# Attention and feed-forward block on one core: the next group's weights are prepared by a table of slots

## What is computed

```python
ln = layernorm(layernorm(x)) * ln_w + ln_b
q, k, v = fp8_linear(ln, wq), fp8_linear(ln, wk), fp8_linear(ln, wv)   # each input divided by its scale, clipped, rounded to fp8
qx      = fp8_linear(ln, wqx)
kx, vx  = split(ctx @ w_kv_x.T)                                        # cross attention on the context
q, k, qx, kx = ln_over_128_columns(each head)
core = softmax(q k^T / sqrt(128)) v ;  xout = softmax(qx kx^T / sqrt(128)) vx   # 8 groups, 2 heads of each kind in a group
x = x + fp8(concat(core, xout) / proj_smooth) @ wproj.T * scales
x = x + (silu(z @ gate.T) * (z @ up.T)) @ down.T,  z = layernorm(x)    # int weights, zero point 128
```

## Time and profile before

| | |
|---|---|
| median of three runs | 1833.42 us (1830.92 to 1835.13) |
| the profiled execution's own time | 1835.97 us |
| its span, first to last instruction | 1834.1 us |
| mean granted TensorE clock | 0.973 |
| busy: PE, DVE, ACT, POOL | 1655.5, 1364.6, 1403.9, 1086.3 us |
| one group of 64 slots in the middle | 164.8 us |

### The profile page before, as it was taken

One profiled execution on the slowest core, in us unless ns is written; L12 is line 12 of the kernel. 1 busy time (PEld: TensorE's weight loads), 2 busy tenths in 40 slices (PEclk: granted clock), 3 DMA queues, 4 the chain that ended last, 5 costly groups with the idle time before them and its releaser, 6 DMA issues. The chain is left out here.

```text
span 1834.1 us, 43340 instructions
## 1 busy us (share of the span) xinstructions
PE 1655.5 (90%) x15491; PEld 1237.8 (67%) x15776; DVE 1364.6 (74%) x3172; ACT 1403.9 (77%) x2936; POOL 1086.3 (59%) x1022
## 2 busy tenths in 40 slices
PE   1459999999999999999999999999998479999999
PEld 1337788778778877887887788778776334444444
DVE  8988988997898899889879988998777432323232
ACT  6669999999999999999999999999999343031211
POOL 1147777777777777777777777777777203030202
PEclk9769999999999999999999999999999789999999
DMA  5028768978787787888778778877889980021100
GB/s 167 24 69 139 139 129 161 145 137 141 142 150 133 142 155 148 134 149 158 125 145 154 136 131 160 153 133 131 172 161 178 279 297 1 25 114 69 68 23 23
DMA packets 641005, 240.32 MB, mean 131 GB/s; under 512 B 612640, under 2 KB 612640, under 8 KB 640800
## 3 DMA queue, kind: packets, MB, share of 16 engines
q1 hardware_dynamic: 640800, 237.66, 64.1%
HBM read 65.58 MB, written 20.99 MB: 47 GB/s over the span
## 5 line engine op out<-in xcount | busy, mean ns | idle before, releaser
L971 POOL TENSOR_TENSOR local<-local 128x512 bf16<-128x512 f32 x512 | 607.2, 1186 | 339.4 <-ACT local L880 339.4
L578 PE MATMUL ps_pj<-wide 128*128 128x256 bf16 (+1 forms) x5544 | 585.2, 255 | 12.7 <-ACT local L803 10.8
L578 PEld LDWEIGHTS ps_pj<-wide 128*128 128x128 bf16 x5544 | 470.7, 98 | 125.5 <-issue 12.0
L877 ACT ACTIVATE local<-ps_s,neg_max 128x512 f32<-128x512 f32 x512 | 389.6, 761 | 46.9 <-DVE neg_max L1178 45.9
L626 PE MATMUL ps_o<-v_hi,local 128*128 128x129 bf16 x2048 | 379.9, 223 | 31.2 <-DMA local<-local 29.3
L880 ACT ACTIVATE local<-ps_s,neg_max 128x512 bf16<-128x512 f32 x512 | 392.3, 766 | 13.9 <-DMA local<-local 13.9
L1178 DVE TENSOR_REDUCE neg_max<-ps_s 128x1 f32<-128x512 f32 x512 | 345.8, 676 | 53.6 <-PE ps_s L642 51.5
L628 PE MATMUL ps_o<-v_hi,local 128*128 128x129 bf16 x2048 | 379.4, 220 | 0.0
L627 PE MATMUL ps_o<-local 128*128 128x128 bf16 x2048 | 379.1, 219 | 0.0
L803 ACT ACTIVATE local<-ps_pj,head_rstd 128x128 f32<-128x128 f32 x756 | 238.2, 434 | 44.0 <-issue 40.2
L947 POOL TENSOR_TENSOR head_rstd<-sq_sum,minus_half 128x3 f32<-128x3 f32 x256 | 218.5, 854 | 25.0 <-DVE sq_sum L1114 25.0
(11 more groups left out here) (112 smaller groups left out, 2591.6 us busy)
## 6 DMA issues: line engine op xcount, KB each, us to landing
w_raw<-w_group SPq DMA_DIRECT2D x32, 512.0 KB, 4.3
quantised_heads<-local SPq DMA_DIRECT2D x32, 512.0 KB, 3.2
wide<-quantised_heads SPq DMA_DIRECT2D x4, 4096.0 KB, 13.1
local<-local SPq DMA_TRANSPOSE x640, 3.2
wide<-x SPq DMA_DIRECT2D x8, 1024.0 KB, 11.8
local<-ctx_t SPq DMA_DIRECT2D x4, 1024.0 KB, 5.3
w_raw<-w_proj SPq DMA_DIRECT2D x8, 512.0 KB, 4.5
wide<-w_proj SPq DMA_DIRECT2D x4, 1024.0 KB, 6.1
```

The source lines that it names most:

```text
L578: last = mm(dst[:, at:at + n], lhs, w_at(par, part, c, cross * 512 + at, n), start=(k == 0), stop=(k == len(terms) - 1))
L877: a(p_exp[:, u % 2], ps_s[u % 2][:], ACT.Exp, bias=neg_max[:, u % 4:u % 4 + 1])
L971: tt_(pp[:, u % PP_BUFS, 1], p_exp[:, u % 2], pp[:, u % PP_BUFS, 0], ALU.subtract)\
```

## The change

The places of the six steps are now written out in a table. The two pieces of a chunk's scale now have three and four heads (`SCALE_CUTS`) and stand in adjacent slots. No instruction is added or taken away. In slots of a group:

| step | before | after |
|---|---|---|
| load (SyncE) | 0, 10, 20, 30 | 0, 8, 20, 28 |
| sums (VectorE) | 6, 16, 26, 36 | 6, 14, 26, 34 |
| scale, first piece | 10, 20, 30, 40 (4 heads) | 10, 18, 30, 38 (3 heads) |
| scale, second piece | 12, 22, 32, 42 (3 heads) | 11, 19, 31, 39 (4 heads) |
| hi (ScalarE) | 14, 24, 34, 44 | 16, 24, 33, 41 |
| lo (VectorE) | 15, 25, 35, 45 | 19, 27, 35, 43 |

```diff
-        PREP_FIRST, PREP_STEP = 4, 10
-        SUMS_LAG, SCALE_LAG, SCALE_PIECES, W_HI_LAG, W_LO_LAG = 2, 6, 2, 10, 11
+        SCALE_CUTS = (0, 3, 7)
+        PREP = {"load": (0, 8, 20, 28), "sums": (6, 14, 26, 34), "scale0": (10, 18, 30, 38), "scale1": (11, 19, 31, 39),
+                "hi": (16, 24, 33, 41), "lo": (19, 27, 35, 43)}
...
-        def prep_at(slot, lag, last):
-            return [c for c in range(CH) if PREP_FIRST + PREP_STEP * c + lag == slot and not last]
+        def prep_at(slot, step, last):
+            return [c for c in range(CH) if PREP[step][c] == slot and not last]
...
-                    for c in prep_at(slot, -PREP_FIRST, last):
+                    for c in prep_at(slot, "load", last):
                         sp.wait_ge(w_loaded, 16 * (CH * g + CH + c + FREE))
                         sp.wait_ge(w_ready, CH * g + CH + c - 1 + W_FREE)
...
-                    for c in prep_at(slot, W_HI_LAG, last):
+                    for c in prep_at(slot, "hi", last):
                         weight_hi((g + 1) % 2, c, CH * g + CH + c + 1)
...
-                n = 8 // SCALE_PIECES
-                for k in range(n * piece, min(n * (piece + 1), 7)):
+                for k in range(SCALE_CUTS[piece], SCALE_CUTS[piece + 1]):
...
-                    for c in prep_at(slot, SUMS_LAG, last):
+                    for c in prep_at(slot, "sums", last):
                         weight_sums(c, CH * g + CH + c + 1)
...
-                    for piece in range(SCALE_PIECES):
-                        for c in prep_at(slot, SCALE_LAG + 2 * piece, last):
+                    for piece in range(2):
+                        for c in prep_at(slot, f"scale{piece}", last):
                             weight_scale(c, piece, CH * g + CH + c + 1)
-                    for c in prep_at(slot, W_LO_LAG, last):
+                    for c in prep_at(slot, "lo", last):
                         weight_lo((g + 1) % 2, c, CH * g + CH + c + 1)
```

More of the change, by code:

```diff
@@ L1033, in weight_scale @@
                                            ALU.subtract, ALU.mult)
-                if piece == SCALE_PIECES - 1:
+                if piece == 1:
                     last.then_inc(w_scaled, 1)
```

## The result

The changed kernel takes 1840.3 us (median of 11 runs, 1834.59 to 1842.63); the kernel before takes 1832.37 us (median of 11). The ratio is 1.0043, 95% interval 1.0034 to 1.0052: slower by 8 us. The forecast was 5.6 us slower.

A forecast was written before the change was run, and what follows sets the result against it. TensorE, busy for 90% of the span, was taken as the bound. Terms of -1.0, +1.8 and 0.0 us gave +0.8 a group, +5.6 over seven: 1841.6, rounded to 1839 us given the runs' lower median; range 1824 to 1851 us.

The forecast's parts named there:

- the three terms: Changes of a group's first three sixteen-slot stretches: -1.0, +1.8 and 0.0 us, together +0.8 us a group.
- a third stretch that moves by a microsecond: Sign of being wrong: slots 32 to 47, forecast at about 41.3 us, move by a microsecond either way.
- The bound of 3.82 us a group: Preparation in slots 0 to 47 costs 3.82 us a group, so any placement wins at most 26.7 us, 1.5%.
- The low part of slot 19 and the load: VectorE's low part of chunk 0 ends at 672.1 us; chunk 2's load in SyncE's slot 20 waits until then.
- The stall: TensorE begins unit 17's products, in slot 22, 2.9 us later; bounds 0.7 to 5.9 us.
- The rest of the second stretch: Slots 16 to 31: present waits go while TensorE stands, 0.4 of 1.49 us stay; stretch +1.8 us with 2.9 us stall.
- The third stretch: Slots 32 to 47: a gain of 0.6 us and a loss of 0.6 us, together 0.0 us.
- The gain of the copies: ScalarE's copies leave slots 34 and 44 for 33 and 41, mostly idle time: 0.6 us won a group.
- the loss by VectorE's bursts: VectorE's heads, sums and low part crowd slots 30 to 39 without free slots between: 0.6 us lost a group.
- The first stretch: Slots 0 to 15: ScalarE's copy leaves slot 14, ending the wait before slot 16's scores; 1.0 of 1.29 us won.
- The load of slot 28: SyncE's load there waits for chunk 1's low part of slot 27: costed at nothing, 0.5 us if VectorE is behind.

The follow-up runs named there:

- the best: Changed kernel with chunk 2's load in slot 24, chunk 1's second scale piece in 22, its copy in 25 (also chunk 3's load 32, smoothing load 50): 1820.92 (1820.89) us.

## Why the prediction was right

The sign and the main mechanism were forecast: +5.6 us against a measured +8, by way of the load that waits in SyncE's queue. That the size is so near is in part luck. Two of the three terms were off by more than a microsecond a group, in opposite directions, and the group on whose clock they were worked out changed by -1.2 us, not +0.8. The forecast also named as a sign of being wrong a third stretch that moves by a microsecond; it moved by -1.08 us in the mean. Point by point:

- **The bound of 3.82 us a group.** No version came near it; the best, with 1821 us, won some 12 of the 26.7 us. The fourth stretch stayed at 40.26 us.
- **The low part of slot 19 and the load.** Forecast to end 10.8 us after the scores of slot 16 (672.1 - 661.3), measured 10.6, in every group. Two errors cancel here. The four heads began 8.4 us after the scores instead of 7.6, and took 1.10 us instead of 2.0, less than the 1.45 that I had called the least. The transposes behind the load landed after 4.6 us; 4.8 was taken.
- **The stall.** This term was right. Forecast 2.9 us in front of unit 17's products; measured, counted from the scores of slot 16, 2.4 in the fourth group, 2.2 to 3.9 over all seven and 2.85 in the mean of groups 2 to 7, as the landing took 4.5 to 6.6 us. That the load's wait is the cause is shown by the run with the load in slot 24, and that it acts one for one by the run with the second piece in slot 22.
- **The rest of the second stretch.** This step failed. I had "the waits that it has now go too" and counted 1.1 us for them, out of 1.49. By the right boundary there were only 1.07 us of waits in that stretch of the fourth group. In the mean of groups 2 to 7, 0.9 us of the old waits did go, in slots 24, 26 and 31, but as much came in others. Slots 22 and 23 are 1.1 us longer than their shortest length after the change and 0.5 before. In slot 23 TensorE waits for the transposes of unit 19, which stand in the queue behind those that were held up and behind the load of the smoothing rows. The term is +2.84 instead of +1.8.
- **The third stretch.** The gain of the copies was taken as 0.6 us and is 1.5; the loss by VectorE's bursts was taken as 0.6 and is at most 0.45 (42.28 with the old copies, against 41.83 before). The term is -1.08 instead of 0, and it almost cancels the error above. Two slips made it small. The stretch had 1.46 us to lose and not 1.04, and slot 34, which is 2 modulo 8, has a transposed head like slots 14 and 44; the step left it out. Behind that copy lies most of what was won.
- **The first stretch.** The term was right (-1.09 against -1.0), its make-up was not. The step gave all of it to the copy's leaving slot 14. In the means 0.73 us are the wait in front of slot 16's scores, and the rest lies in slots 9, 11 and 14. The run with the loads alone already wins 0.31 us there, with the load of chunk 1 in slot 8, which the step had at nothing. In the wait itself the copy and the low part, which stood beside GpSimd's instruction, both have a share. The copy's leaving may well be enough alone, as the step said: after the change GpSimd's part of the transposed head ends at 661.69, 0.80 us ahead of slot 16's scores (0.05 ahead before), and a GpSimd instruction longer by 0.4 us would still leave 0.4 of that. This is an estimate from the row below; the low part has to follow the copy, so no kernel has the one in 16 and the other in 15.

```profile
660.60 1.09 POOL L955 TENSOR_TENSOR local<-local 128x512 bf16<-128x512 f32 x1
```

- **The load of slot 28.** Costed at nothing; it waits 0.5 to 1.1 us, and TensorE does not wait for it in a way that the stretches show (slot 29 is 0.1 us longer).

What stays open is why the groups differ. The load is issued at the same place in each (10.7 us after the scores of slot 16), but the transposes behind it land after 5.4, 5.0, 4.5, 4.6, 4.6, 5.9 and 6.6 us in groups 1 to 7. The three groups with the slowest landings, 1, 6 and 7, have the longest second stretches (45.6, 45.1 and 46.1 us, against 42.8 to 44.1). What sets the landing time no run shows.

## What to carry to other kernels

A step that is moved has to be followed through every in-order queue that waits for it. Here the burst on VectorE mattered little by itself; but a load whose buffer had been free for 10 us became one that waits 2.7 us, and a transpose with 0.4 us to spare stood behind it. Place such a load where its buffer has been free for some time, and where the transfer behind it has slack. When two steps moved together and a gain is credited to one, move each back alone: here both had a share. And compare group by group, not only one group or the total: here the total was right while the group that was worked out moved the other way.

## What the runs showed of the hardware

In the changed kernel a transpose issued right behind the 512 KB load of slot 20 landed after 4.5 to 6.6 us; the median of all of them was 3.3, with the same bytes. VectorE's and GpSimd's instructions lengthened each other when both read two operands from SBUF: 1.52 for 1.16 us on GpSimd and 2.02 for 1.21 us on VectorE, the longer one being the one that started second. In the changed kernel GpSimd's instruction started 0.19 us behind VectorE's low part of slot 19 (at 671.90) and took 2.04 us:

```profile
672.09 2.04 POOL L972 TENSOR_TENSOR local<-local 128x512 bf16<-128x512 f32 x1 [0.53 <-ACT local L881]
```

The Trainium skill (SBUF — State Buffer, Who interferes with whom) says that a VectorE instruction with two SBUF inputs contends with a GpSimd one that reads SBUF; all three rows agree.
